# Turned queries and keys: two 64-partition sine products on VectorE, one cosine product on GpSimd

## The chip, the cores and the metric

The kernel runs on one core of one Trainium2 chip. The metric is the device time of one launch in microseconds, as the median of the runs. The profile is one further execution, recorded by the hardware profiler. The engines are TensorE (PE, with its weight load PEld), VectorE (DVE), ScalarE (ACT), GpSimd (POOL) and SyncE (SP).

## What is computed

One transformer layer over 2 x 1024 tokens of 256 channels, in float32: attention with 16 query heads and 4 key/value heads of 128, a layer norm of input plus attention, a mixture of 64 experts (6 for each token) with two shared ones, and a second layer norm. The change touches only the rotary turning of queries and keys in the attention:

```python
def _rotate_half(x):
    d = x.shape[-1] // 2
    return jnp.concatenate([-x[..., d:], x[..., :d]], axis=-1)
...
q = q * cos + _rotate_half(q) * sin
k = k * cos + _rotate_half(k) * sin
...
scores = jnp.einsum('bqhd,bkhd->bhqk', q, k) * scale
scores = jnp.where(causal[None, None], scores, jnp.finfo(scores.dtype).min)
attn = jax.nn.softmax(scores, axis=-1)
out = jnp.einsum('bhqk,bkhd->bqhd', attn, v).reshape(b, s, NH * HD)
```

Queries and keys lie turned on the chip: the 128 channels of a head on the partitions, 512 tokens along the row. The half rotation therefore swaps partitions 0 to 63 with 64 to 127.

## The kernel before

`attention` goes through 4 rounds of 64 steps. A step `n` takes one block of 128 queries of one head, for which `key_tiles(n)` key tiles of 128 count: 1 to 4 in the first 16 steps of every 32, 5 to 8 in the other 16. Every float32 matrix is split into a high part (rounded to fp32r, by ACT) and a low part (the rest), and each product is made of three matmuls: high by high, high by low, low by high.

Each engine has its own program, a loop over the steps written out by hand, and runs it in order; semaphores tie the engines together. In step `n` PE makes the scores of `n` (L606 to L611), transposes the probabilities of `n - 2` (L620), sums half of the outputs of a pair of blocks (the products of L539 to L541 into `o_ps`), and then has one "filling" of the single bank `proj_ps` (`fill`, L561, the same three lines): a projection of keys (K), queries (Q) or values (T), the turning back of values (V), or the output projection (O). `FILLS` gives the steps: modulo 16, K is filled at step 7, T at 3, V at 11; modulo 4, Q at 2, O at 0 and 1. The next filling waits until the bank is empty (`bank_free`): after O for `resid_added` (L504), after V for `v_split` (L516), after K and Q for `proj_taken` (L401). The outputs of step `n` (even) wait for `o_split` (`o_lo`, L476) and for `pt_split` (`pt_lo`, L468).

The turning of a K or Q filled at step `n`:

- ACT copies `proj_ps` to `taken` in step `n + 1` (L401).
- POOL multiplies `taken` by `cos` in step `n + 1` with two products of 64 partitions that swap the halves (L347, L349), so `turned` lies with its halves swapped; the weights that use it are swapped alike, on both sides of the scores, which leaves the scores as they are. Then POOL waits for the sine product and adds it (L353).
- DVE multiplies all 128 partitions of `taken` by `sin` in step `n + 2` (L490).
- ACT rounds `turned` to `q_hi` or `k_hi` in step `n + 3` (L428), and POOL makes `q_lo` or `k_lo` (L333).

DVE's order in a step is: `pt_lo` of step `n - 3` (L468); in even steps `o_lo` (L476); if `n % 4 == 1` the reciprocal of the row sums (L482); the sine product of a K or Q (L490); the two residual instructions of an O (L501); the maximum of the scores of `n` (L508); the low part of a V (L514). ACT's exponential (L391) needs the maximum, PE's transposes need the exponential. K's sine falls on step 9 of 16, Q's on every fourth step from 0, V's low part on step 12.

Of the kernel before, what the change touches and what calls it, by code (L numbers as in the profile page):

```python
# [26 lines left out]
ALU = mybir.AluOpType  # L27
ACT = mybir.ActivationFunctionType
AX = mybir.AxisListType
# [119 lines left out]
def now(k, per, n):  # L149


    return (k + 1) * per + n
# [10 lines left out]
def attention(nc, dram, resid, consts):  # L163
    with ExitStack() as ctx:
# [135 lines left out]
        def _(pool):  # L300
# [3 lines left out]
            pool.sem_inc(cos_made, 2 * len(ROPES))  # L304
            pool.sem_inc(turn_made, len(ROPES))
            pool.sem_inc(turn_split, len(ROPES))
            made = {"turn": len(ROPES), "split": len(ROPES)}
            for name, positions in (("x", SPLIT_X), ("w", SPLIT_W), ("wo", SPLIT_WO)):

                made[name] = SPLITS + sum(runs(at(positions, n), SPLITS, True, False) for n in range(FIRST, FIRST + STEPS))  # L310
# [14 lines left out]
            def body(k, first, last):  # L325
                for n in range(FIRST, FIRST + STEPS):
                    use = fill_at(n - 3)
                    if use and use[0] in "KQ" and runs(use[1], per(use[0]), first, last):

                        r = rope_of(*use)  # L330
                        hi, lo = turned_into(*use)
                        pool.wait_ge(turn_hi_made, now(k, len(ROPES), r + 1))
                        nc.gpsimd.tensor_tensor(lo, turned[r % 2][:], hi.bitcast(F32), ALU.subtract).then_inc(turn_split, 1)  # L333
                        made["split"] += 1
                    use = fill_at(n - 1)
                    if use and use[0] in "KQ" and runs(use[1], per(use[0]), first, last):

                        r = rope_of(*use)
                        pos = slice(half(*use) * HALF, (half(*use) + 1) * HALF)
                        pool.wait_ge(proj_taken, now(k, len(ROPES), r + 1))  # L340
                        pool.wait_ge(turn_made, made["turn"])
                        pool.wait_ge(turn_split, made["split"])
                        if not first:
                            pool.wait_ge(x_split, made["x"])
                            pool.wait_ge(w_split, made["w"])
                            pool.wait_ge(wo_split, made["wo"])
                        nc.gpsimd.tensor_tensor(turned[r % 2][0:64], taken[r % 2][64:128], cos[64:128, pos], ALU.mult).then_inc(cos_made, 1)  # L347
                        pool.wait_ge(cos_made, 2 * now(k, len(ROPES), r) + 1)
                        nc.gpsimd.tensor_tensor(turned[r % 2][64:128], taken[r % 2][0:64], cos[0:64, pos], ALU.mult).then_inc(cos_made, 1)  # L349
                        pool.wait_ge(cos_made, 2 * now(k, len(ROPES), r + 1))  # L350
                        made["turn"] += 1
                        pool.wait_ge(sin_made, now(k, len(ROPES), r + 1))
                        nc.gpsimd.tensor_tensor(turned[r % 2][:], turned[r % 2][:], turn_sin[r % 2][:],  # L353
                                                ALU.add).then_inc(turn_made, 1)
                    if not first:
                        lower_parts(pool, nc.gpsimd, k, n, first, last)
                        for name, positions in (("x", SPLIT_X), ("w", SPLIT_W), ("wo", SPLIT_WO)):
                            made[name] += runs(at(positions, n), SPLITS, first, last)
# [90 lines left out]
        def _(dve):  # L449
# [8 lines left out]

            def body(k, first, last):
                for n in range(FIRST, FIRST + STEPS):  # L460
# [11 lines left out]
                    if n % 2 == 0 and runs(j, PAIRS, first, last):  # L472
# [4 lines left out]
                                                ALU.subtract).then_inc(o_split, 1)  # L477
                    q = (n - 5) // 4
# [4 lines left out]
                    use = fill_at(n - 2)  # L483
                    if use and use[0] in "KQ" and runs(use[1], per(use[0]), first, last):

                        r = rope_of(*use)
                        pos = slice(half(*use) * HALF, (half(*use) + 1) * HALF)
                        dve.wait_ge(proj_taken, now(k, len(ROPES), r + 1))
                        dve.wait_ge(turn_made, now(k, len(ROPES), r - 1))
                        nc.vector.tensor_tensor(turn_sin[r % 2][:], taken[r % 2][:], sin[:, pos], ALU.mult).then_inc(sin_made, 1)  # L490
# [14 lines left out]
                    if runs(n, STEPS, first, last):  # L505

                        dve.wait_ge(scored, now(k, STEPS, n + 1))
                        nc.vector.tensor_reduce(neg_max[:, n % 4:n % 4 + 1], scores_ps[n % 2][:, score_cols(n)],  # L508
                                                AX.X, ALU.max, negate=True).then_inc(max_made, 1)
                    if use and use[0] == "V" and runs(use[1], per("V"), first, last):  # L510
# [5 lines left out]
                                                ALU.subtract).then_inc(v_split, 1)  # L516
                    if first:

                        lower_parts(dve, nc.vector, k, n, first, last)
# [947 lines left out]
```

## Time and profile before

| | us |
|---|---|
| median of 3 runs | 1422.31 |
| lowest, highest | 1422.07, 1423.52 |
| profiled execution | 1425.77 |
| its span in the trace | 1424.0 |
| PE busy | 1254.1 (88%) |
| DVE busy | 991.5 (70%) |
| ACT busy | 846.5 (59%) |
| POOL busy | 809.8 (57%) |

The attention lies in the first 60% of the span, the routing and the experts behind it. PE busy is the time in which a matmul was under way, with modelled ends; the pitch of the matmuls' starts says more of what PE did. A timeline lists an engine's instructions by start and duration; in square brackets stands idle time of the engine before the instruction, and what ended it. Instructions of DVE can start a little before their predecessor's recorded end.

### The profile page before, as it was taken

How to read it: one execution, taken by the hardware profiler on the slowest of the kernel's cores; microseconds unless marked ns; L12 is line 12 of the kernel's file. 1: busy time of each engine (PE TensorE's matmuls, PEld its weight loads, DVE VectorE, ACT ScalarE, POOL GpSimd, SP SyncE). 2: the span in 40 equal slices, each digit the busy share in tenths (PEclk: the TensorE clock that was granted, in tenths of full speed). 3: DMA queues.
4: the chain of work that ended last, by engine and by line, in shares of the span. 5: the costliest groups of instructions: out<-in, count | busy, mean ns of one | idle time of the engine just before them, and what ended most of it. 6: DMA issues, size and time to landing. Idle time of an engine off the chain costs nothing. (4 is left out here: it accounts for less than half of the span.)

```text
span 1424.0 us, 27954 instructions
## 1 busy us (share of the span) xinstructions
PE 1254.1 (88%) x8732; PEld 1117.1 (78%) x8732; DVE 991.5 (70%) x2012; ACT 846.5 (59%) x1875; POOL 809.8 (57%) x798
## 2 busy tenths in 40 slices
PE   3899999999999999999999997539925999999966
PEld 2789899899899899899899897536615999999954
DVE  2677677677677677777776777572204999999956
ACT  2666666566666566666665664622204989899932
POOL 4754754654754654754654630037774888888840
PEclk9999999999999999999999999559966999999979
DMA  6320040120040120140400001014225888888868
GB/s 224 116 76 1 11 153 23 57 76 1 21 151 15 57 76 1 27 150 11 122 1 2 1 1 34 1 49 104 104 101 172 263 260 262 257 263 263 267 204 269
DMA packets 100293, 151.29 MB, mean 106 GB/s; under 512 B 10410, under 2 KB 73038, under 8 KB 100196
## 3 DMA queue, kind: packets, MB, share of 16 engines
q1 hardware_dynamic: 89156, 124.75, 29.0%
q0 software_dynamic: 11040, 25.30, 5.3%
q8 instruction: 54, 0.88, 0.3%
q14 instruction: 43, 0.35, 0.1%
HBM read 92.51 MB, written 62.46 MB: 109 GB/s over the span
## 5 line engine op out<-in xcount | busy, mean ns | idle before, releaser
L508 DVE TENSOR_REDUCE neg_max<-scores 128x1 f32<-128x256 f32 (+7 forms) x256 | 192.6, 752 | 178.3 <-PE scores L611 178.1
L418 ACT ACTIVATE pt_hi<-pt 128x512 fp32r<-128x512 f32 (+3 forms) x384 | 174.8, 490 | 204.8 <-PE pt L620 201.7
L468 DVE TENSOR_TENSOR pt_lo<-pt,pt_hi 128x512 fp32r<-128x512 f32 (+3 forms) x384 | 200.8, 551 | 23.5 <-ACT pt_hi L418 21.6
L391 ACT ACTIVATE probs<-scores,neg_max 128x256 f32<-128x256 f32 (+7 forms) x256 | 190.1, 743 | 21.9 <-DVE neg_max L508 21.8
L539 PE MATMUL o_ps<-pt_hi,v_hi 128*128 128x256 f32 (+1 forms) x640 | 193.4, 302 | 4.9 <-DVE o_lo L476 4.8
L347 POOL TENSOR_TENSOR turned<-taken,cos 64x512 f32<-64x512 f32 x80 | 105.6, 1320 | 152.7 <-ACT taken L401 147.5
L540 PE MATMUL o_ps<-pt_lo,v_hi 128*128 128x256 f32 (+1 forms) x640 | 179.5, 281 | 0.0
L541 PE MATMUL o_ps<-pt_hi,v_lo 128*128 128x256 f32 (+1 forms) x640 | 179.1, 280 | 0.0
L620 PE MATMUL pt<-ident,probs 128*128 128x128 f32 x1152 | 168.2, 273 | 0.0
L1106 POOL DMA_INDIRECT results_dram<-y_sb,dest x134 | 145.2, 1083 | 32.8 <-issue 25.9
L611 PE MATMUL scores<-k_hi,q_lo 128*128 128x512 f32 (+4 forms) x384 | 151.5, 395 | 0.0
L333 POOL TENSOR_TENSOR q_lo<-turned,q_hi 128x512 fp32r<-128x512 f32 x64 | 82.6, 1291 | 113.9 <-ACT q_hi L428 113.9
L353 POOL TENSOR_TENSOR turned<-turned,turn_sin 128x512 f32<-128x512 f32 x80 | 103.8, 1298 | 72.7 <-DVE turn_sin L490 71.2
L752 POOL DMA_INDIRECT rows_dram<-rows,slots_int x96 | 94.2, 982 | 86.0 <-issue 86.0
L620 PEld LDWEIGHTS pt<-ident,probs 128*128 128x128 f32 x1152 | 134.9, 141 | 5.0
L606 PE MATMUL scores<-k_hi,q_hi 128*128 128x512 f32 (+4 forms) x384 | 132.1, 344 | 2.7 <-POOL q_lo L333 2.7
L607 PE MATMUL scores<-k_lo,q_hi 128*128 128x512 f32 (+4 forms) x384 | 131.1, 341 | 0.0
L539 PEld LDWEIGHTS o_ps<-pt_hi,v_hi 128*128 128x128 f32 x640 | 121.1, 189 | 10.2 <-issue 7.4
L540 PEld LDWEIGHTS o_ps<-pt_lo,v_hi 128*128 128x128 f32 x640 | 121.9, 191 | 0.0
L541 PEld LDWEIGHTS o_ps<-pt_hi,v_lo 128*128 128x128 f32 x640 | 121.2, 189 | 0.0
L501 DVE SCALAR_TENSOR_TENSOR resid<-proj_ps,row_inv,resid 128x256 f32<-128x256 f32 x256 | 110.7, 473 | 7.5 <-PE proj_ps L541 7.5
L349 POOL TENSOR_TENSOR turned<-taken,cos 64x512 f32<-64x512 f32 x80 | 105.8, 1323 | 6.3
(186 smaller groups left out, 3619.0 us busy)
## 6 DMA issues: line engine op xcount, KB each, us to landing
rows_dram<-empty SPq DMA_DIRECT2D x32, 919.1 KB
up_raw<-in_up SPq DMA_DIRECT2D x69, 368.0 KB, 3.9
x_in<-rows_dram SPq DMA_DIRECT2D x68, 258.0 KB, 3.5
parts<-results_dram SPq DMA_DIRECT2D x16, 768.0 KB, 9.8
down_raw<-in_down SPq DMA_DIRECT2D x69, 128.0 KB
down_raw<-in_down_tail SPq DMA_DIRECT2D x69, 112.0 KB
w_raw<-in_w SPq DMA_DIRECT2D x8, 768.0 KB, 9.1
x_raw<-in_xT SPq DMA_DIRECT2D x8, 512.0 KB, 5.0
```

The lines of the kernel that those rows point to most:

```text
L391: nc.scalar.activation(probs[:, m % 4, 0:w], scores_ps[m % 2][:, score_cols(m)], ACT.Exp, bias=neg_max[:, m % 4:m % 4 + 1], accum_out=row_ ...
L418: nc.scalar.activation(pt_hi[m // 2 % 2][:, a:z, P * (m % 2):P * (m % 2) + P], pt_ps[c % 2][:, 0:P * (z - a)].rearrange("p (k q) -> p k q" ...
L468: nc.vector.tensor_tensor(pt_lo[m // 2 % 2][part], pt_ps[c % 2][:, 0:P * (z - a)].rearrange("p (k q) -> p k q", q=P), pt_hi[m // 2 % 2][pa ...
L508: nc.vector.tensor_reduce(neg_max[:, n % 4:n % 4 + 1], scores_ps[n % 2][:, score_cols(n)], AX.X, ALU.max, negate=True).then_inc(max_made, 1)
L539: nc.tensor.matmul(out, lh, rh, start=first, stop=False)
L540: nc.tensor.matmul(out, lh, rl, start=False, stop=False)
L541: return nc.tensor.matmul(out, ll, rh, start=False, stop=last)
L606: nc.tensor.matmul(out, q_hi[b][qt], k_hi[u][:, keys], start=True, stop=False)
L607: nc.tensor.matmul(out, q_hi[b][qt], k_lo[u][:, keys], start=False, stop=False)
L611: mm = nc.tensor.matmul(out, q_lo[b][qt], k_hi[u][:, keys], start=False, stop=True)
L620: mm = nc.tensor.transpose(pt_ps[c % 2][:, (t - a) * P:(t - a + 1) * P], probs[:, m % 4, t * P:(t + 1) * P], ident[:])
L1106: pool.indirect_dma_start(out=dram["results"], out_offset=bass.IndirectOffsetOnAxis(ap=dest[buf][:, s:s + 1], axis=0), in_=y_sb[buf][:, s, ...
```

## The change

The sine products swap the halves and the cosine product does not, so `turned` lies straight. POOL makes one cosine product of 128 partitions in place of two of 64. DVE makes two sine products of 64 partitions in place of one of 128, each from the opposite half of `taken` and of `sin`. In DVE's order within a step, Q's sine keeps its place (the reciprocal now stands behind it, which never falls on the same step), K's sine moves behind the residual and the low part of V, and the maximum moves behind the low part of V and K's sine. POOL's extra waits for earlier sums and low parts are replaced by one wait on `turn_split`.

```diff
-            pool.sem_inc(cos_made, 2 * len(ROPES))
-            pool.sem_inc(turn_made, len(ROPES))
-            pool.sem_inc(turn_split, len(ROPES))
-            made = {"turn": len(ROPES), "split": len(ROPES)}
...
+            for s in (cos_made, turn_made, turn_split):
+                pool.sem_inc(s, len(ROPES))
...
                         pool.wait_ge(proj_taken, now(k, len(ROPES), r + 1))
-                        pool.wait_ge(turn_made, made["turn"])
-                        pool.wait_ge(turn_split, made["split"])
-                        if not first:
-                            pool.wait_ge(x_split, made["x"])
-                            pool.wait_ge(w_split, made["w"])
-                            pool.wait_ge(wo_split, made["wo"])
-                        nc.gpsimd.tensor_tensor(turned[r % 2][0:64], taken[r % 2][64:128], cos[64:128, pos], ALU.mult).then_inc(cos_made, 1)
-                        pool.wait_ge(cos_made, 2 * now(k, len(ROPES), r) + 1)
-                        nc.gpsimd.tensor_tensor(turned[r % 2][64:128], taken[r % 2][0:64], cos[0:64, pos], ALU.mult).then_inc(cos_made, 1)
-                        pool.wait_ge(cos_made, 2 * now(k, len(ROPES), r + 1))
-                        made["turn"] += 1
+                        pool.wait_ge(turn_split, now(k, len(ROPES), r - 1))
+                        nc.gpsimd.tensor_tensor(turned[r % 2][:], taken[r % 2][:], cos[:, pos], ALU.mult).then_inc(cos_made, 1)
+                        pool.wait_ge(cos_made, now(k, len(ROPES), r + 1))
                         pool.wait_ge(sin_made, now(k, len(ROPES), r + 1))
...
+            def turn_by_sine(k, kind, i):
+
+                r = rope_of(kind, i)
+                pos = slice(half(kind, i) * HALF, (half(kind, i) + 1) * HALF)
+                dve.wait_ge(proj_taken, now(k, len(ROPES), r + 1))
+                dve.wait_ge(turn_made, now(k, len(ROPES), r - 1))
+                nc.vector.tensor_tensor(turn_sin[r % 2][0:64], taken[r % 2][64:128], sin[64:128, pos], ALU.mult)
+                nc.vector.tensor_tensor(turn_sin[r % 2][64:128], taken[r % 2][0:64], sin[0:64, pos],
+                                        ALU.mult).then_inc(sin_made, 1)
+
...
+                    turn = fill_at(n - 2)
+                    if turn and turn[0] == "Q" and runs(turn[1], per("Q"), first, last):
+                        turn_by_sine(k, *turn)
                     q = (n - 5) // 4
...
-                    use = fill_at(n - 2)
-                    if use and use[0] in "KQ" and runs(use[1], per(use[0]), first, last):
-
-                        r = rope_of(*use)
-                        pos = slice(half(*use) * HALF, (half(*use) + 1) * HALF)
-                        dve.wait_ge(proj_taken, now(k, len(ROPES), r + 1))
-                        dve.wait_ge(turn_made, now(k, len(ROPES), r - 1))
-                        nc.vector.tensor_tensor(turn_sin[r % 2][:], taken[r % 2][:], sin[:, pos], ALU.mult).then_inc(sin_made, 1)
...
                         ins.then_inc(resid_added, 1)
-                    if runs(n, STEPS, first, last):
-
-                        dve.wait_ge(scored, now(k, STEPS, n + 1))
-                        nc.vector.tensor_reduce(neg_max[:, n % 4:n % 4 + 1], scores_ps[n % 2][:, score_cols(n)],
-                                                AX.X, ALU.max, negate=True).then_inc(max_made, 1)
...
+                    if turn and turn[0] == "K" and runs(turn[1], per("K"), first, last):
+                        turn_by_sine(k, *turn)
+                    if runs(n, STEPS, first, last):
+
+                        dve.wait_ge(scored, now(k, STEPS, n + 1))
+                        nc.vector.tensor_reduce(neg_max[:, n % 4:n % 4 + 1], scores_ps[n % 2][:, score_cols(n)],
+                                                AX.X, ALU.max, negate=True).then_inc(max_made, 1)
```

## Rows read from the trace of the kernel before

**Rows 1.** The page: busy time of each engine; PE's busy tenths in 40 slices.

```profile
PE 1254.1 (88%) x8732; PEld 1117.1 (78%) x8732; DVE 991.5 (70%) x2012; ACT 846.5 (59%) x1875; POOL 809.8 (57%) x798
...
PE   3899999999999999999999997539925999999966
```

**Rows 2.** The waits of PE, 25 to 880 us: total us, times, longest.

```profile
PE proj_ps L539 <- DVE v_lo L514: 11.9, 9, 1.4
PE proj_ps L539 <- DVE resid L501: 5.2, 8, 0.7
```

**Rows 3.** The timeline of PE in a light half: start us, duration us, engine, line.

```profile
267.94 0.27 PE L541 MATMUL o_ps<-pt_hi,v_lo 128*128 128x128 f32 x1
268.87 0.39 PE L539 MATMUL proj_ps<-wo_hi,o_hi 128*128 128x256 f32 x1 [0.65 <-DVE resid L501]
...
270.36 0.36 PE L539 MATMUL o_ps<-pt_hi,v_hi 128*128 128x256 f32 x1
...
277.30 0.39 PE L539 MATMUL proj_ps<-wo_hi,o_hi 128*128 128x256 f32 x1 [1.31 <-DVE v_lo L514]
```

**Rows 4.** The timeline of DVE over the same steps, 8 to 12.

```profile
264.59 1.45 DVE L490 TENSOR_TENSOR turn_sin<-taken,sin 128x512 f32<-128x512 f32 x1
...
267.06 0.96 DVE L490 TENSOR_TENSOR turn_sin<-taken,sin 128x512 f32<-128x512 f32 x1
267.95 0.86 DVE L501 SCALAR_TENSOR_TENSOR resid<-proj_ps,row_inv,resid 128x256 f32<-128x256 f32 x2
268.74 0.41 DVE L508 TENSOR_REDUCE neg_max<-scores 128x1 f32<-128x256 f32 x1
269.06 0.67 DVE L468 TENSOR_TENSOR pt_lo<-pt,pt_hi 128x512 fp32r<-128x512 f32 x1
269.66 0.41 DVE L476 TENSOR_TENSOR o_lo<-o_ps,o_hi 128x256 fp32r<-128x256 f32 x1
...
274.83 0.42 DVE L476 TENSOR_TENSOR o_lo<-o_ps,o_hi 128x256 fp32r<-128x256 f32 x1 [0.21 <-ACT o_hi L382]
275.17 1.27 DVE L490 TENSOR_TENSOR turn_sin<-taken,sin 128x512 f32<-128x512 f32 x1
276.37 0.28 DVE L508 TENSOR_REDUCE neg_max<-scores 128x1 f32<-128x128 f32 x1
276.57 0.68 DVE L514 TENSOR_TENSOR v_lo<-proj_ps,v_hi 128x512 fp32r<-128x512 f32 x1
```

**Rows 5.** The timeline of POOL over the same steps.

```profile
264.20 1.29 POOL L349 TENSOR_TENSOR turned<-taken,cos 64x512 f32<-64x512 f32 x1
266.18 1.29 POOL L353 TENSOR_TENSOR turned<-turned,turn_sin 128x512 f32<-128x512 f32 x1 [0.69 <-DVE turn_sin L490]
267.61 1.55 POOL L347 TENSOR_TENSOR turned<-taken,cos 64x512 f32<-64x512 f32 x1
...
274.62 1.28 POOL L347 TENSOR_TENSOR turned<-taken,cos 64x512 f32<-64x512 f32 x1 [0.22 <-issue]
```

**Rows 6.** The timeline of DVE in the experts: full and 48-partition instructions.

```profile
1161.38 0.41 DVE L1262 TENSOR_TENSOR hidden<-silu,gate_up 128x256 f32<-128x256 f32 x1
...
1163.36 0.43 DVE L1276 TENSOR_TENSOR hidden_hi<-hidden,hidden_hi 48x256 fp32r<-48x256 f32 x1
1163.82 0.69 DVE L1241 TENSOR_TENSOR xt_lo<-x_ps,xt_hi 128x512 fp32r<-128x512 f32 x1
```

**Rows 7.** The timeline of DVE in a heavy half, step 12.

```profile
332.17 0.68 DVE L490 TENSOR_TENSOR turn_sin<-taken,sin 128x512 f32<-128x512 f32 x1
```

**Rows 8.** The timeline of PE in the same heavy half.

```profile
334.51 0.28 PE L539 MATMUL proj_ps<-wo_hi,o_hi 128*128 128x256 f32 x1
```

**Rows 9.** The timeline of PE at the start of the attention.

```profile
34.22 0.47 PE L606 MATMUL scores<-k_hi,q_hi 128*128 128x128 f32 x1 [2.70 <-POOL q_lo L333]
...
41.93 0.50 PE L539 MATMUL proj_ps<-x_hi,w_hi 128*128 128x512 f32 x1 [0.72 <-ACT taken L401]
...
47.93 0.36 PE L539 MATMUL o_ps<-pt_hi,v_hi 128*128 128x256 f32 x1 [1.25 <-DVE o_lo L476]
```

More of the change, by code:

```diff
@@ L303, in _ @@
             pool.sem_inc(wo_split, SPLITS)
-            pool.sem_inc(cos_made, 2 * len(ROPES))
-            pool.sem_inc(turn_made, len(ROPES))
-            pool.sem_inc(turn_split, len(ROPES))
-            made = {"turn": len(ROPES), "split": len(ROPES)}
-            for name, positions in (("x", SPLIT_X), ("w", SPLIT_W), ("wo", SPLIT_WO)):
-                made[name] = SPLITS + sum(runs(at(positions, n), SPLITS, True, False) for n in range(FIRST, FIRST + STEPS))
+            for s in (cos_made, turn_made, turn_split):
+                pool.sem_inc(s, len(ROPES))
             pool.memset(ident[:], 0.0).then_inc(const_step, 1)
@@ L333, in body @@
                         nc.gpsimd.tensor_tensor(lo, turned[r % 2][:], hi.bitcast(F32), ALU.subtract).then_inc(turn_split, 1)
-                        made["split"] += 1
                     use = fill_at(n - 1)
@@ L356, in body @@
                         lower_parts(pool, nc.gpsimd, k, n, first, last)
-                        for name, positions in (("x", SPLIT_X), ("w", SPLIT_W), ("wo", SPLIT_WO)):
-                            made[name] += runs(at(positions, n), SPLITS, first, last)
             run_rounds(pool, body)
```

## The prediction

> **What bounds the kernel now.** I read the page first. TensorE (PE) is busy 88% of the span and 9 tenths or more in nearly every slice of the first 60% [rows 1]; that stretch, up to some 870 us, is the attention, and the change lies in it alone. So PE is the limit there, and a cost on VectorE (DVE) or GpSimd (POOL) counts only where it opens or closes a gap of PE, and the second view is the list of PE's waits in the attention [rows 2]: 11.9 us before a filling that waits for the low part of the values (L514), 5.2 us before one that waits for the residual (L501), nearly all else small. Third, PE's timeline. It repeats every 105.9 us: 16 steps over 1 to 4 key tiles (I call them the light half), then 16 over 5 to 8 (the heavy half). The heavy halves have no gap. Each of the eight light halves has four: 0.22 us at its step 6, 0.65 us at step 9 (residual), 1.31 us at step 12 (low values), 0.22 us at step 14; [rows 3] has the second and third, and where PE takes up the outputs of step 10 (270.36). The fourth view is the DVE and POOL timelines of the same microseconds, to see what makes these two gaps [rows 4, 5].
>
> At step 9 DVE runs reciprocal, the keys' sine (267.06 to 268.02), then the residual (to 268.81), and PE's second output filling starts at 268.87. At step 12 it runs the output's low part (to 275.25), a query sine of 1.27, a maximum of 0.28, then the low values (to 277.25), and PE starts at 277.30 [rows 3, 4].
>
> **The price of a sine product.** Alone it takes 0.68 [rows 7]. Beside a POOL product it is held up: at 264.59 the sine found a cosine running that ended at 264.20 + 1.29 = 265.49, and itself ended at 264.59 + 1.45 = 266.04, 0.55 later; at 267.06 it found the sum that ended at 266.18 + 1.29 = 267.47, and ended at 268.02, again 0.55 later [rows 4, 5]. So a sine that meets a running POOL product ends 0.55 after that one's end. The Trainium skill has a rule for this that speaks against the change (SBUF — State Buffer, "Who interferes with whom"): a VectorE instruction with two SBUF inputs and a GpSimd instruction that reads SBUF exclude one another for the whole instruction, and who issues first wins. The trace agrees except in the size: by the rule's letter the sine would need its whole 0.68 after the other's end, which would add 0.13 for each one blocked, 1 us in all below.
>
> **Half the partitions do not halve it.** On DVE, 48 partitions by 256 take 0.43 against 0.41 for 128 by 256 [rows 6]; on POOL, 64 partitions by 512 take 1.28 to 1.29, as 128 by 512 do [rows 5]. So I take 0.68 for each of the two sine products, and 1.29 for the one cosine that replaces two. There is also a hand-over. Ordinarily a DVE instruction starts 0.08 before its predecessor's end (276.57, behind a maximum that ended at 276.37 + 0.28 = 276.65). Where the starting partition changes it starts behind it: the 48-partition instruction that writes from partition 64 ends at 1163.36 + 0.43 = 1163.79, and the next starts at 1163.82 [rows 6]. The pair changes it three times, so from one instruction's end to the next one's start it takes 0.01 + 0.68 + 0.01 + 0.68 + 0.03 = 1.41, where one unblocked sine takes 0.68 - 0.16 = 0.52. The added 0.89 has as its lower bound a pair that costs as one does now (0), as upper bound two blocked products.
>
> **Query sines (64 of them).** They keep their place. In a light half's step 8, and where else the second cosine used to block them, the pair costs what the blocked one did: from 264.67 to 266.05 with no POOL product beside it, since POOL will have made its only cosine by 264.20, where its second one began; the old sine ended at 266.04. At steps 0 and 4 the pair delays a maximum by 0.2 to 0.9; ScalarE (ACT) then has idle time before its next copy, and the DVE stands idle 0.2 to 2 us within the next steps, so it is taken in. In the heavy half the DVE idles up to 2.9 us in a step. Its tightest place is the low values: sines unblocked from 332.25 on (the present one starts 0.08 before its predecessor's end), to 333.63, then 0.68 to 334.34 since the maximum now stands behind; PE wants them at 334.51 [rows 7, 8]. No gap, by 0.17.
>
> **Keys' sine in the light half, step 9 (8 times).** This decides. Taking it out from ahead of the residual ends the residual at 267.07 + 0.86 = 267.93, before PE asks for it at 267.94 + 0.27 = 268.21: the gap of 0.65 closes. But the pair now stands between the residual and the maximum, and behind that are two things that PE needs for its next outputs: a low part of the probabilities and o_lo. POOL's order is the query's sum (266.18 to 267.47, as before, since the query's sine ends as before), then the keys' cosine, 267.61 to 268.90. The first keys' product, ready at 267.94, finds it running: 268.90 + 0.55 = 269.45. The second: 270.14. Maximum 0.41 with its hand-over: 270.58. Low part of the probabilities 0.67, starting 0.08 early: 271.17. o_lo 0.41: 271.51. PE then starts its outputs at 271.54; it did at 270.36 [rows 3, 4]. So 0.65 is won at step 9, 1.83 is lost at step 10: **+1.18** each. Nothing gives it back: PE has no slack in which a delay can vanish. Bounds: if the pair were not blocked, 267.94 + 1.37 = 269.31, and the same chain ends at 270.71 (+0.35); if both were blocked, +0.6 more.
>
> **Low values, step 12 (8 times).** Out of its way goes a maximum of 0.28, and in its way comes one more sine. Its block vanishes too: POOL's cosine started only at 274.62 [rows 5], behind the keys' low part, and held the sine; with one cosine less per turn and PE 1.18 later, it ends before the DVE arrives. In PE's time: 275.25, products to 275.94 and 276.63, low values 276.66 to 277.34, PE at 277.39, against 277.30: **+0.09**. Bounds -0.2 (no hand-overs) and +0.6 (blocked).
>
> **The start (once).** Until the first scores PE waits for POOL's turning of the first queries, 2.70 us, and then for 0.72 and 1.25 more behind chains through POOL and ACT [rows 9]. One cosine (1.29) less in each of the first turns, minus blocked sines, makes the first sum end about 0.7 and the second about 2 us earlier. Of that little reaches PE at once: a sine pair ahead of the first maximum holds that to its old time within 0.15. At the gap of 0.72 the copy is then ready (-0.85 with it), at that of 1.25 a quarter is won. **-1.1**, bounds 0 and -3. The waits that POOL loses are met without stall in the rows I read; I count nothing.
>
> **Sum.** 8 x (1.18 + 0.09) - 1.1 = +9.1 us. The profiled execution took 1425.77 (1424.0 of span and 1.8 around it), 3.5 above the median of 1422.31; the same addition gives 1434.9 for such a one, and 1431.4 on the median.
>
> **Rivals.**
> A, the keys' pair is not held up (POOL's cosine comes earlier or lets it through): 8 x (0.35 + 0.09) - 1.1 = +2.4, 1424.7. For it: the pair misses the cosine's start by only 0.33 us. Against: three blocked sines in the rows, each by an instruction that had started first (the third: cosine to 275.90, sine to 276.44).
> B, the other side: a narrow product is short and passes the port. If it takes 0.34, the pair costs one present sine. Then step 10 starts as ACT allows, about 0.32 before 270.36, and the low values start when their high part is there, 0.6 earlier: 8 x -0.92 - 1.1 = -8.5, 1413.8. It decides from below some 0.45 us for one product. Against it are the rows of 48 and 64 partitions.
> C, the pair costs more than I count (both blocked, or a dearer hand-over), 0.3 for each: then the light half loses 0.6 more, and the heavy half's low values, with 0.17 to spare, open a gap of 0.13: 8 x 0.73 = +5.8 more, 1437.2.
>
> **Chances.** Forecast 0.60 (its own range 1428.5 to 1434), A 0.18, B 0.08, C 0.14. The range 1423.5 to 1436 leaves out B and the upper part of C. About 0.2%, 2.8 us, is what a measurement of this kernel can tell from no change: faster 0.09 (B and a little of A), same 0.19 (A and the foot of the forecast), slower 0.72.
>
> **What would show it.** In the profile after: the sine line with 160 instructions near 0.68, one of them near 1.5 in each light half, at step 9; the wait for the residual gone from PE's list; the wait for o_lo or the probabilities' low part at step 10 near 1.8 us, eight times; the wait for the low values still some 1.3. I am wrong if the step 10 gap is below 1 us (A), if sine products of 64 partitions take clearly less than 0.68 (B), or if heavy halves show gaps (C).

## The result, and the profile after the change

| | before | after |
|---|---|---|
| median of four runs, us | 1422.91 (1422.07 to 1424.34) | 1445.38 (1442.94 to 1447.28) |
| ratio, 95% interval | | 1.015 (1.0139 to 1.0162) |
| profiled execution, us (its span) | 1425.77 (1424.0) | 1442.94 (1441.2) |
| VectorE (DVE) busy, us | 991.5 | 1031.1 |
| GpSimd (POOL) busy, us | 809.8 | 700.7 |
| last maximum of the attention starts at, us | 869.22 | 888.77 |

The change costs 22.5 us on the medians, where +9.1 was forecast. The direction was right, the forecast size was 40% of the measured one, and 1445.38 lies outside the range, which ended at 1436.

The page after says where not to look. Its engine row answers to that in [rows 1]:

```profile
PE 1260.4 (87%) x8732; PEld 1120.1 (78%) x8732; DVE 1031.1 (72%) x2092; ACT 851.5 (59%) x1875; POOL 700.7 (49%) x718
```

POOL has 80 instructions and 109 us less, DVE 80 instructions and 40 us more, TensorE (PE) the same 8732 matmuls. Yet PE's busy time went up by 6.3 us: the same matmuls became longer. That one number is the first sign of what the prediction left out.

**The gaps.** The list of PE's waits, 100 to 850 us, which holds seven light halves (total us, times, longest). Before:

```profile
PE proj_ps L539 <- DVE v_lo L514: 9.2, 7, 1.3
PE proj_ps L539 <- DVE resid L501: 4.5, 7, 0.7
PE o_ps L539 <- DVE o_lo L476: 3.1, 14, 0.2
```

After:

```profile
PE o_ps L530 <- DVE o_lo L470: 15.7, 21, 1.8
PE proj_ps L530 <- DVE v_lo L498: 10.2, 7, 1.5
PE proj_ps L530 <- DVE resid L490: 1.1, 7, 0.2
```

The residual's wait of 0.65 at step 9 is gone, as forecast. In its place stands one of 1.80 for the output's low part at step 10: 15.7 - 3.1 = 12.6 us in seven halves. The low values at step 12 went from 1.31 to 1.46. And a wait of 0.17 for a residual is new. PE's gaps in one repeat of 32 steps are now 0.22 + 1.80 + 1.46 + 0.22 + 0.17 = 3.87 us, against 0.22 + 0.65 + 1.31 + 0.22 = 2.40 before: +1.47 each. The last of them, 0.17, stands at step 17, the second step of the heavy half.

**The chain behind the large gap.** Timeline of DVE after (start us, duration us, engine, line); it answers to [rows 4]:

```profile
269.25 0.86 DVE L490 SCALAR_TENSOR_TENSOR resid<-proj_ps,row_inv,resid 128x256 f32<-128x256 f32 x2
270.14 1.35 DVE L449 TENSOR_TENSOR turn_sin<-taken,sin 64x512 f32<-64x512 f32 x1
271.51 0.69 DVE L450 TENSOR_TENSOR turn_sin<-taken,sin 64x512 f32<-64x512 f32 x1
272.23 0.42 DVE L506 TENSOR_REDUCE neg_max<-scores 128x1 f32<-128x256 f32 x1
272.57 0.68 DVE L462 TENSOR_TENSOR pt_lo<-pt,pt_hi 128x512 fp32r<-128x512 f32 x1
273.17 0.41 DVE L470 TENSOR_TENSOR o_lo<-o_ps,o_hi 128x256 fp32r<-128x256 f32 x1
```

Timeline of POOL at the same time, behind the queries' sum:

```profile
269.67 1.28 POOL L336 TENSOR_TENSOR turned<-taken,cos 128x512 f32<-128x512 f32 x1
```

The first product of the keys starts while the cosine runs, which ends at 269.67 + 1.28 = 270.95, and ends itself at 270.14 + 1.35 = 271.49, 0.54 later. The second takes 0.69, and the maximum, the probabilities' low part and o_lo follow without a hole until 273.58. PE takes up the outputs at 273.73. This is the chain that the prediction wrote down, instruction by instruction.

**What was not in it.** PE in the same step, after, across the gap and beyond:

```profile
273.73 0.36 PE L530 MATMUL o_ps<-pt_hi,v_hi 128*128 128x256 f32 x1 [1.80 <-DVE o_lo L470]
...
274.52 0.47 PE L530 MATMUL proj_ps<-x_hi,w_hi 128*128 128x512 f32 x1
274.79 0.63 PE L531 MATMUL proj_ps<-x_lo,w_hi 128*128 128x512 f32 x1
```

The same matmuls in the kernel before:

```profile
271.15 0.40 PE L539 MATMUL proj_ps<-x_hi,w_hi 128*128 128x512 f32 x1
271.39 0.40 PE L540 MATMUL proj_ps<-x_lo,w_hi 128*128 128x512 f32 x1
```

Matmuls of 128x512 start 0.24 apart and last 0.40 before; after, they last 0.63, and the seven from 274.79 to 277.35 start 0.42 to 0.43 apart. The clock that TensorE was granted explains it. The page does not show it: its row for the granted clock, in tenths over 40 slices of 36 us, reads 9 for nearly the whole attention in both kernels, since a fall of 3.4 us takes only 0.05 from a slice (before, then after):

```profile
PEclk9999999999999999999999999559966999999979
PEclk8999999999999999999999999559976999999979
```

Windows view after (stretch, its length, busy us of PE, PEld, DVE, ACT, POOL with counts, then the granted clock as a share of full speed, DMA share, GB/s):

```profile
56.00:60.00 4.00, 3.02 (x17) 2.44 (x18) 2.28 (x6) 2.57 (x7) 3.36 (x3) 1.00 0.74 204
274.00:278.00 4.00, 4.00 (x16) 2.92 (x14) 1.03 (x3) 1.60 (x4) 2.26 (x3) 0.59 0.00 0
383.00:387.00 4.00, 4.00 (x16) 2.96 (x15) 1.11 (x4) 1.69 (x4) 2.38 (x3) 0.62 0.00 0
...
820.00:824.00 4.00, 4.00 (x29) 3.40 (x29) 1.88 (x5) 2.32 (x6) 2.92 (x3) 1.00 0.02 4
```

Column PEclk is the reading: 0.59 and 0.62 where it was 1.00 at the same place before. PE is busy all 4.00 us in the last three rows, but makes 16 matmuls in two of them and 29 in the third. Behind the 1.8 us gap the clock goes down from 2.4 to 1.2 GHz for 3.4 us and comes back. It does so in six of the eight light halves of this execution (from about 165, 275, 384, 493, 602 and 712 us), and not in the first and the last, whose gap is as long. Before, it never does between 40 and 880 us. From one light half to the next the work repeats every 105.9 us before, every 107.5 after where the clock holds (105.9 and 1.47 make 107.4), and every 109.1 to 109.2 where it falls, so a fall costs 1.6 to 1.7 us, half of the 3.4 that it lasts.

**The account**, on the last maximum of the attention in the two profiled executions. The start of the attention came out 2.5 us earlier. The gaps add 8 x 1.47 = 11.8. Six falls of the clock add 6 x 1.7 = 10.2. Sum +19.5; the trace has 888.77 - 869.22 = +19.55. (Taken from the repeats instead, 1.6 for each gap sum and 1.6 for each fall, the same account gives +19.9.) The rest of the program, which the change does not touch, was 2.4 us shorter in this one execution, which makes +17.2 on the spans.

### The profile page after: what moved, and what is told of

It is laid out like the page before. It is cut to its first block and busy times, and to the rows that moved or that the text cites. A ratio compares the mean times of both kernels' runs of the same rounds, so it can differ in the third digit from the quotient of the medians.

```text
span 1441.2 us, 27801 instructions
## 1 busy us (share of the span) xinstructions
PE 1260.4 (87%) x8732; PEld 1120.1 (78%) x8732; DVE 1031.1 (72%) x2092; ACT 851.5 (59%) x1875; POOL 700.7 (49%) x718
## 5 line engine op out<-in xcount | busy, mean ns | idle before, releaser
L336 POOL TENSOR_TENSOR turned<-taken,cos 128x512 f32<-128x512 f32 x80 | 104.2, 1302 | 162.0 <-ACT taken L385 162.0
L530 PE MATMUL proj_ps<-x_hi,w_hi 128*128 128x512 f32 x192 | 81.2, 423 | 16.4 <-DVE w_lo L251 12.4
```

The source lines that it names most:

```text
L530: nc.tensor.matmul(out, lh, rh, start=first, stop=False)
```

## The experiments

Gaps are PE's, in one light half, by step. On the chip of the first four runs the kernel before took 1493.79 us, because the part behind the attention was some 70 us longer there (623.8 us behind the last maximum in the trace of the order alone, 554.8 in that of before). The attention was not: with the order alone its last maximum comes 2.7 us before that of before. The changed kernel itself was not run on that chip. So for these runs the ratio and the gaps are what can be compared. "Last maximum" always stands against 869.22.

### The products alone, in the old order

```diff
                     turn = fill_at(n - 2)
-                    if turn and turn[0] == "Q" and runs(turn[1], per("Q"), first, last):
-                        turn_by_sine(k, *turn)
...
                         nc.vector.reciprocal(row_inv[:, cols], row_sum[:, cols]).then_inc(inv_made, 1)
+                    if turn and turn[0] in "KQ" and runs(turn[1], per(turn[0]), first, last):
+                        turn_by_sine(k, *turn)
```

(The maximum moves back ahead of the low values too.)

> The changed products (two sines of 64 partitions, one cosine) in VectorE's order of before: keys' pair ahead of the residual, maximum ahead of the low values. Theory 1 (stall plus clock): what costs is where the keys' pair stands and that GpSimd holds it up, and a PE gap near 2 us lets TensorE's granted clock fall to half for some 3.4 us, another 1.7 us. Here the pair stands before the residual: first product held by GpSimd's sum (to 268.0 in the microseconds of before), second by the cosine (to 269.7), residual to 270.6, so a gap near 2.3 at step 9 and none at step 10: 1.7 us per light half more than before, 0.4 more at the low values, and the clock falls in 6 to 8 light halves: 1445 to 1453 us. Theory 2 (the order is what costs, the products are free): within 1 us of before, 1423. Theory 3 (the products cost by VectorE's load, wherever they stand): as the changed kernel, 1445, with the gap spread over several steps.

Measured: 1530.55, ratio 1.0244 (1.0211 to 1.0276). The list of PE's waits, 100 to 850 us:

```profile
PE proj_ps L528 <- DVE resid L490: 18.5, 13, 2.5
PE proj_ps L528 <- DVE v_lo L503: 15.1, 14, 1.7
PE o_ps L528 <- DVE o_lo L470: 2.7, 12, 0.2
```

And the keys' pair (DVE) with PE behind it:

```profile
387.59 0.90 DVE L449 TENSOR_TENSOR turn_sin<-taken,sin 64x512 f32<-64x512 f32 x1
388.50 1.66 DVE L450 TENSOR_TENSOR turn_sin<-taken,sin 64x512 f32<-64x512 f32 x1
...
391.12 0.39 PE L528 MATMUL proj_ps<-wo_hi,o_hi 128*128 128x256 f32 x1 [2.50 <-DVE resid L490]
```

Here both products are held up, the first by POOL's sum, the second by its cosine (0.90 and 1.66), which was the prediction's upper bound for a pair. The gap of step 9 is 2.50 and that of step 12 is 1.65; a heavy half has one of 0.50 for the low values, where [rows 8] had none. So the two products are the dear part of the change, and the new order makes them cheaper than they would be. The clock falls here nine times: behind the 2.50 gap in six of eight cases, and behind the 1.65 gap in three of eight. The account closes again: the waits of 100 to 850 us sum to 36.3 us here and 16.8 before, 2.79 more in each light half, so 8 x 2.79 + 9 x 1.7 - 0.8 (start) = +36.8; the last maximum is at 906.10, +36.9. Theory 1 had the place and nearly the size of the large gap (2.3), but not the falls behind the gap of 1.65 nor the gap in the heavy half, and +2.4% is above the +1.6 to +2.2% that its times stood for. Theories 2 and 3 are out.

### The order alone, with the old products

```diff
-                    use = fill_at(n - 2)
-                    if use and use[0] in "KQ" and runs(use[1], per(use[0]), first, last):
+                    turn = fill_at(n - 2)
+                    if turn and turn[0] == "Q" and runs(turn[1], per(turn[0]), first, last):
...
+                    turn = fill_at(n - 2)
+                    if turn and turn[0] == "K" and runs(turn[1], per(turn[0]), first, last):
```

> The kernel before with the new order alone: one sine of 128 partitions, two cosines; keys' sine behind the residual, maximum behind the low values. Theory 1: the single keys' sine meets the first cosine, ends at 269.45, o_lo at 270.8, so a gap of 1.1 at step 10 in place of 0.65 at step 9; low values earlier by 0.2; the clock stays up, as it did in before at gaps of 1.3: 8 x 0.3 = +2.4, 1423 to 1427 us. Theory 2 (the order costs): near the changed kernel, 1440 to 1446, with a gap of 1.8 at step 10. Theory 3: as before, 1423.

Measured: 1492.56, ratio 0.9998 (0.9989 to 1.0008), no difference. Waits of PE, 100 to 850 us, and the keys' sine:

```profile
PE o_ps L547 <- DVE o_lo L476: 10.9, 21, 1.1
PE proj_ps L547 <- DVE v_lo L509: 5.2, 7, 0.7
...
371.58 1.60 DVE L519 TENSOR_TENSOR turn_sin<-taken,sin 128x512 f32<-128x512 f32 x1
```

Gaps: none at step 9, 1.12 at step 10, 0.74 at step 12: 2.30 in all against 2.40. The last maximum is 2.7 us earlier, 2.0 of it from the start and 0.1 from each repeat. Theory 1 had the gap at step 10 right; what it put at 0.2 for the low values came out as 0.57, and with it the +2.4 us went. The order swaps a wait of 0.65 for one of 1.12, and gains 0.57 at step 12. Even one sine behind the residual is held up by a cosine (1.60). The clock never falls in the attention from 40 us on. The two halves of the change are therefore about nothing for the order, and +2.4% for the products, which the order brings down to +1.5%.

### The step 10 gap filled with matmuls

```diff
-                        for c0, c1 in spans:
+                        for c0, c1 in spans * (4 if n % 32 == 10 else 1):
```

The scores of step 10 are computed four times over, some 2 us of needless PE work exactly where PE stands idle.

> The changed kernel, and in step 10 of each light half PE makes the scores of the block four times in place of once, each time from the start, so the output is the same. That is some 1.7 us of additional matmuls, put where PE stands idle for 1.8 us. Theory 1: the idle time goes, nothing is later, the granted clock stays at full speed and the matmuls of steps 10 and 11 keep their pitch: 10 to 14 us less than the changed kernel, 1431 to 1436 us, although PE does more. Rival (the clock falls for another reason, as the load of all engines or a fixed interval): the clock falls as often as in the changed kernel and the time is 1444 to 1448.

Measured: 1506.65, ratio 1.0087 (1.007 to 1.0104), against 1.015 and 1.0137 for the changed kernel itself. PE's waits, then two windows of 6 us across the place where the clock fell:

```profile
PE o_ps L530 <- DVE o_lo L470: 3.1, 14, 0.2
...
171.00:177.00 6.00, 4.68 (x35) 4.23 (x36) 5.19 (x13) 3.47 (x9) 4.91 (x3) 1.00 0.20 35
275.00:281.00 6.00, 4.54 (x37) 4.00 (x36) 4.66 (x10) 3.28 (x9) 2.56 (x2) 1.00 0.00 1
```

The gap is gone, the clock holds from 40 us on, and by its ratio the kernel with more work is half a percent faster: 12.9 us above before, within the 9 to 14 that theory 1 gave, where the changed kernel was 22.5 and 18.5 above on its two chips. The last maximum comes 10.7 us after that of before, 1.6 for each light half with 2.1 off at the start: as a step 10 that is just as late, without the fall. This separates the two costs. The delay of step 10 is DVE's chain and stays when PE is kept busy; the rest of the loss hangs on PE standing idle.

### The same, half as much

```diff
-                        for c0, c1 in spans:
+                        for c0, c1 in spans * (2 if n % 32 == 10 else 1):
```

> As the run that made the scores of step 10 four times, but twice: some 0.55 us more matmuls, so PE idles about 1.25 us there, with everything else of the changed kernel. Theory 1: the clock stays up, and the light half costs nothing more than in the changed kernel less the 1.7 us of the slow matmuls. Rival: any idle time beyond that of before lets the clock fall; then it falls as often as in the changed kernel.

Measured, one run: 1436.44 against 1424.35. PE's waits:

```profile
PE o_ps L530 <- DVE o_lo L470: 11.3, 21, 1.2
```

The gap is 1.17, the clock does not fall, and the last maximum comes at +11.4, about 1.6 for each half. The delay is that of the changed kernel, and only the idle part of it is shorter.

### The changed kernel once more

The same kernel without an edit, on another chip, to see whether the falls are a property of a place in the program.

> The changed kernel once more, beside the kernel before on the same chip, as the measure for the two that follow. Expected: gaps of 1.8 us at step 10 of all eight light halves, a fall of the granted clock behind at least five of them, and 1.3 to 1.6% over before.

Measured: 1442.89 (1440.57 to 1447.49), ratio 1.0137 (1.0115 to 1.016). The gaps are the same (PE's waits), and the windows behind two of them are not:

```profile
PE o_ps L530 <- DVE o_lo L470: 15.8, 21, 1.8
...
276.00:280.00 4.00, 4.00 (x15) 2.88 (x15) 0.79 (x3) 1.27 (x3) 2.71 (x3) 0.60 0.00 0
384.00:388.00 4.00, 3.61 (x22) 3.05 (x23) 2.10 (x6) 2.18 (x6) 3.32 (x4) 1.00 0.00 0
```

The clock fell behind three of the eight gaps (at 168, 277 and 601 us), where it was six the first time; at least five were expected. The light half at 384 had a fall in one execution and none in the other. So a fall follows a gap of this length in some cases, in varying places. The account: start -0.9, gaps +11.8, three falls +5.1, sum +16.0; measured 885.73 - 869.22 = +16.5. A varying number of falls would also make the runs of this kernel spread more, and they do: 7 us here and 4 in the first comparison, against 2.2 to 2.3 for the kernel before in both comparisons. That the falls are what spreads them is not shown, since only one execution on each chip has a trace.

### The keys' product made narrow

```diff
-                        turn_by_sine(k, *turn)
+                        turn_by_sine(k, *turn, width=8 if n % 32 == 9 else HALF)
```

The keys' sine products of the light halves cover 8 of 512 columns; the other 504 are left out.

> The changed kernel, with the keys' two sine products of the light halves (step 9) on 8 of their 512 columns: 504 columns of the keys' sine product are left out there. Theory 1: the gap at step 10 goes from 1.8 to 0.2 to 0.4, the clock does not fall: 8 x 1.5 + 10 to 14 us less than the changed kernel, 1418 to 1423 us; the low values' gap stays near 1.45. Theory 3 (load of VectorE by all the pairs): most of the loss stays, 1435 to 1445, since 64 of 80 pairs are as in the changed kernel.

Measured: 1497.63, ratio 1.002 (1.001 to 1.003). POOL's cosine, the pair, and PE at step 10:

```profile
373.91 1.29 POOL L336 TENSOR_TENSOR turned<-taken,cos 128x512 f32<-128x512 f32 x1
374.38 0.85 DVE L449 TENSOR_TENSOR turn_sin<-taken,sin 64x8 f32<-64x8 f32 x1
375.24 0.16 DVE L450 TENSOR_TENSOR turn_sin<-taken,sin 64x8 f32<-64x8 f32 x1
376.93 0.35 PE L530 MATMUL o_ps<-pt_hi,v_hi 128*128 128x256 f32 x1 [0.77 <-DVE o_lo L470]
```

The gap falls from 1.80 to 0.77, and the clock holds in all eight halves, so the keys' pair makes the larger part of this gap, and theory 3 is out. But a gap of 0.2 to 0.4 was expected, and 1418 to 1423 us where before had 1422.3; the ratio stands 0.2% above 1. The expectation took nearly the whole of the pair's time as gone, and the first product, narrow as it is, still waits for the cosine, which ends at 375.20. This shows the hold-up by itself: the free narrow product takes 0.16, the one behind the cosine 0.85, so the hold-up costs 0.69. For the full product it costs 1.35 - 0.69 = 0.66, so it has little to do with its size. The gap of 1.46 at step 12 stays, as it should.

### POOL's cosine behind the keys' products

```diff
                         pool.wait_ge(turn_split, now(k, len(ROPES), r - 1))
+                        if use[0] == "K":
+                            pool.wait_ge(sin_made, now(k, len(ROPES), r + 1))
                         nc.gpsimd.tensor_tensor(turned[r % 2][:], taken[r % 2][:], cos[:, pos], ALU.mult).then_inc(cos_made, 1)
```

> The changed kernel; GpSimd's cosine product of the keys now waits for VectorE's two sine products of the keys, so they can't be held up by it (the cosine itself and the sum come about 0.6 us later). This prices the hold-up: the forecast put it at 0.83 us per light half (+1.18 held up, +0.35 not). Theory 1: the gap at step 10 goes from 1.8 to 1.0 to 1.1, the clock stays up (it stayed up at gaps of 1.1 to 1.5 in the runs so far): 8 x 0.8 + 10 to 14 us less than the changed kernel, 4 to 8 us over before. Rival: the hold-up isn't what fills the gap, the gap stays above 1.6 and the time within 3 us of the changed kernel.

Measured: 1430.09 (1428.97 to 1431.72), ratio 1.0038 (1.0024 to 1.0052). DVE, POOL and PE:

```profile
375.81 0.69 DVE L451 TENSOR_TENSOR turn_sin<-taken,sin 64x512 f32<-64x512 f32 x1
376.51 0.68 DVE L452 TENSOR_TENSOR turn_sin<-taken,sin 64x512 f32<-64x512 f32 x1
...
377.37 1.27 POOL L338 TENSOR_TENSOR turned<-taken,cos 128x512 f32<-128x512 f32 x1 [1.99 <-DVE turn_sin L452]
...
378.73 0.36 PE L532 MATMUL o_ps<-pt_hi,v_hi 128*128 128x256 f32 x1 [1.13 <-DVE o_lo L472]
```

Both products are free, the gap of step 10 is 1.13, and the clock does not fall. The hold-up is worth 1.81 - 1.13 = 0.68 for each light half, where the sum of the prediction had 0.83; the pair, even free, behind the residual costs the rest. With one wait, 12.8 us of the changed kernel's loss are gone: 8 x 0.68 = 5.4 of it is the shorter gap. The other 7.4 lie between what three falls and six falls of 1.7 us cost (5.1 and 10.2), and the time is in the 4 to 8 us over before that theory 1 gave.

### The keys' turning taken apart and made later

The runs so far say what is wanted: the new order, no hold-up, and POOL's work of the keys out of step 9. This version takes the old products in the new order; the keys' first cosine waits for their sine, the second cosine and the sum go behind the queries' low part, one step later, and k_hi and k_lo two steps later.

```diff
-                    use = fill_at(n - 3)
-                    if use and use[0] in "KQ" and runs(use[1], per(use[0]), first, last):
+                    for kind, back in (("Q", 3), ("K", 3 if first else 5)):
+                        use = fill_at(n - back)
+                        if use and use[0] == kind and runs(use[1], per(kind), first, last):
...
+                        if kind == "K" and not first:
+                            pool.wait_ge(sin_made, now(k, len(ROPES), r + 1))
+                        if 0 in halves:
+                            nc.gpsimd.tensor_tensor(turned[r % 2][0:64], taken[r % 2][64:128], cos[64:128, pos], ALU.mult).then_inc(cos_made, 1)
+                        if 1 in halves:
```

> A version meant to beat both. The products of before (one sine of 128 partitions, two cosines), the new order of VectorE, and the keys' turning taken apart so that it is in nobody's way: GpSimd's first cosine of the keys waits for VectorE's sine (no hold-up), the second cosine and the sum come behind the queries' low part, and ScalarE's rounding and GpSimd's low part of the keys come two steps later (step 12 in place of 10). Expected: gap at step 10 from 1.1 (with the new order alone) to 0.2 to 0.3, low values' gap 0.8 to 1.1: 0.7 us less than before per light half and 2 us less at the start, if that holds: 1 to 6 us under before. Rival: the later sum of the keys pushes GpSimd's next cosine or ScalarE's copies into the way, and the low values' gap or the wait for the queries' low part grows by as much: within 1 us of before.

Measured: 1421.52 (1418.7 to 1423.44, ten runs) against 1424.35, ratio 0.9979 (0.997 to 0.9989). PE's waits, 100 to 850 us:

```profile
PE proj_ps L560 <- DVE v_lo L522: 8.7, 7, 1.3
PE o_ps L560 <- DVE o_lo L489: 4.6, 21, 0.2
```

Steps 6, 10 and 14 have 0.22 each, step 12 has 1.25: 1.91 against 2.40 before. It is faster than the kernel before by 0.2%, which is small, but its interval leaves out 1. The low values' gap came out above the 0.8 to 1.1 expected, the time within the range. One fall of the clock is in its attention from 40 us on, at 64 us, behind a low-values gap that was 1.61 long in this first half. The account: 8 x -0.49 - 2.1 (start) + 1.7 (one fall) + 0.36 (that longer gap) = -4.0; measured 865.22 - 869.22 = -4.0. Some 1.2 of the start's 2.1 belong to this execution and not to the kernel: the next version differs from this one nowhere before step 11, and its step 8 comes only 0.8 earlier than before (see on the start below). The medians, -2.8 us, carry the result.

### The same with the queries' cosine of step 11 behind its sine

Against the version before this one:

```diff
-                        if kind == "K" and not first:
+                        if (kind == "K" or n % 16 == 11) and not first:
```

> The version before this one (keys turned late), and GpSimd's cosine products of the queries filled at step 10 wait for VectorE's sine of step 12, so that the sine, and the low values behind it, are not held up. In the trace of that version the sine ends at 380.34 in place of 379.61 and the low values 0.6 us later than they could. Theory: the gap at step 12 goes from 1.25 to 0.7, the queries' sum comes some 0.8 us later and makes ScalarE's rounding and the outputs of step 14 late by 0.2 to 0.4: 0.2 to 0.4 us less per light half, 1 to 3 us below that version, 0.3 to 0.4% below before. Rival: the later sum makes step 14's gap (0.22) grow by 0.5 or more: no gain.

Measured: 1424.25 against 1424.02, ratio 1.0004 (0.9995 to 1.0014). PE's waits:

```profile
PE o_ps L560 <- DVE o_lo L489: 11.4, 21, 1.2
PE proj_ps L560 <- DVE v_lo L522: 5.2, 7, 0.7
```

Step 12 went from 1.25 to 0.74, and step 14 from 0.22 to 1.20. The wait bought 0.51 and cost 0.98 two steps later. The chain to it, POOL's sum for the queries, then ACT and DVE:

```profile
383.52 1.29 POOL L365 TENSOR_TENSOR turned<-turned,turn_sin 128x512 f32<-128x512 f32 x1
384.91 0.63 ACT L441 ACTIVATE q_hi<-turned 128x512 fp32r<-128x512 f32 x1 [0.87 <-POOL turned L365]
385.84 0.42 DVE L489 TENSOR_TENSOR o_lo<-o_ps,o_hi 128x256 fp32r<-128x256 f32 x1 [1.08 <-ACT o_hi L394]
```

The held-back cosines make the sum late, ACT stands idle 0.87 us for it, and o_hi, which is behind q_hi in ACT's order, and with it o_lo and the outputs are late. That is the expectation's mechanism, but with the rival's size; the rival came out, and the version before this one stays the best.

## Why the prediction was right in part, and wrong in size

**The keys' pair at step 9: right.** The residual's gap closed (0.65 to 0). The forecast lost 1.83 at step 10; the gap is 1.80 (1.80 to 1.82 in every light half of both traces of this kernel). The first product ends 0.54 after the cosine where 0.55 was read from three blocked sines. Rival A, that the pair is not held up, is shut out by the 1.35 of its first product. Undoing the hold-up alone gave 0.68, where the sum had 1.18 - 0.35 = 0.83, so with a free pair the gap is 1.13 where the bound gave 1.00.

**No halving: right.** A free product of 64 partitions takes 0.69 on DVE, the one cosine of 128 partitions on POOL 1.28. Rival B is out.

**The low values: right in kind, 0.15 instead of 0.09.** Together with the keys' pair that is +1.30 against +1.27.

**The query sines "taken in": failed at one place.** The prediction called the low values the tightest place of the heavy half, with 0.17 to spare. Those held; the gap opened elsewhere, at the residual behind the pair of step 16, which I had not laid on the timeline. There was no slack there: before, DVE's residual ended at 288.68 + 0.84 = 289.52 and PE took it at 289.57, as soon behind it as at step 9, where PE stood waiting (268.81 and 268.87). After, a query pair with its second product at 291.96 and its maximum at 292.68 goes ahead of it:

```profile
291.96 0.69 DVE L450 TENSOR_TENSOR turn_sin<-taken,sin 64x512 f32<-64x512 f32 x1
...
293.96 0.85 DVE L490 SCALAR_TENSOR_TENSOR resid<-proj_ps,row_inv,resid 128x256 f32<-128x256 f32 x2
294.87 0.39 PE L530 MATMUL proj_ps<-wo_hi,o_hi 128*128 128x256 f32 x1 [0.17 <-DVE resid L490]
```

From the end of o_lo to the start of the maximum the pair takes 1.46 with its hand-overs where the blocked sine took 1.27; with no slack, the 0.19 more is nearly all in the gap of 0.17 that the trace shows, eight times: 1.3 us in all. A gap in the heavy half was one of the prediction's signs of rival C. Its cause is not that of C, a pair dearer by 0.3: this one takes 1.46 where 1.41 was counted. The wrong step was that a query pair costs what the blocked sine before it did.

**The start: right sign, size unsettled.** Forecast -1.1. The maximum of step 8 came 2.5 us earlier in the first trace of the changed kernel and 0.9 earlier in the second. The two differ in the clock and not in the kernel: in the first, matmuls of 128x512 start 0.23 us apart from 16.3 to 19.6 us, the high level, and in the second, as in the kernel before, 0.43 apart there and on to about 39 us, the low level. The two other traces with such an early high stretch, the order alone and the best version, start 2.0 and 2.1 us earlier; of the six others five start 0.7 to 1.3 earlier, around the forecast, and one 2.1. So part of the first trace's 2.5 is probably the early clock and not the change; no run separates them.

**The step that failed: "Nothing gives it back", and with it the sum 8 x (1.18 + 0.09) - 1.1.** They priced a gap of PE at its own length and looked only for what could make it shorter. They named nothing that could make it dearer: the clock granted behind it stood in the sum at nothing, without a reason. The lengths of the gaps account for 11.8 - 2.5 = +9.3 at the last maximum, next to the forecast of +9.1; that near match is partly luck, since it has 1.3 for the residual of step 17 against a start that was earlier than forecast. What is missing is the granted clock: 10.2 us in one trace, 5.1 in the other. In the kernel before the clock held from 40 to 880 us with gaps of up to 1.32; the forecast made a gap of 1.83, longer than any in that stretch, and I did not ask what the clock would do. The 2.70 of [rows 9] is longer still, but it is no evidence for a clock that holds: it stands at 34 us, where TensorE was at the low level already (128x512 matmuls 0.43 apart until 39.4 us, 0.23 from 39.8 us). The range was too narrow for the same reason: it took in the bounds of DVE's times and none for PE's.

The experiments bear this cause out from four sides. (Falls and gaps are counted from 40 us on.) Filling the gap with needless matmuls ends the falls and takes the ratio from 1.0137 or 1.015 to 1.0087. Filling it in part, in one run, does the same to the falls. Making it shorter from DVE's side (0.77 with a narrow product, 1.13 with the cosine behind) does too. And where gaps are longer (2.50 and 1.65 in the old order), there are nine falls. Counted over all traces: behind gaps of 1.6 to 2.5 us the clock fell in 6 of 8, 3 of 8, 6 of 8, 3 of 8 and 1 of 1 cases; behind gaps of up to 1.46 us, which stand eight times in each of six traces, in none. The Trainium skill says (TensorE: Matmul & The Clock Gate, "What's actually happening") that the clock follows how busy the engine has lately been, with the low level as the default. The traces agree in that every one of the 19 falls begins within 1.6 us of the end of a gap of 1.6 us or more, and in that all traces begin at the low level (128x512 matmuls 0.43 us apart at 13 us); which of two equal gaps brings a fall, that sentence does not tell.

**Against the medians.** The attention gives about +16 to +20 us in the two traces of this kernel, the medians +22.5 on one chip and +18.5 on the other. Some 2 to 3 us more are not placed: the profiled execution of the first comparison was itself the fastest of its four, and the number of falls varies from one execution to the next.

**Open.** Why the clock falls behind one gap of 1.8 us and not behind the next. Of the low values' 1.25 us in the best version 0.51 is a sine that is held up; what could take away the other 0.74 was not tried. The changed kernel's own products in the schedule of the best version were not tried.

## What to carry to other kernels

A gap of the bound engine has a second price beside its length. Where a change makes one on TensorE longer than any that the trace of before shows at the high clock, put a fall of the granted clock into the sum, with the extra time that the matmuls behind it would take at half speed, or at least into the range; and read the clock in windows of a few us, since the tenths of the page did not show six falls. And where a GpSimd product holds up a VectorE one, the cost is nearly the rest of the running one (0.66 and 0.69 of 0.8 us here) and hardly depends on the size of the one that waits; an added wait on GpSimd can let the other by first, but look at who needs the product that it holds back, since the wait won 12.8 us at one place here and moved a gap by two steps at another. Last, work "taken in" by idle time must be laid on the timeline at every step that it touches; the place with 0.17 of slack held, the one with none did not.

## What the runs showed of the hardware that I had not expected

- With an idle gap of 1.80 us in otherwise full work, the granted clock went from 2.4 to 1.2 GHz in 6 of 8 and in 3 of 8 cases, at about 1.7 us each. With gaps of 1.46 and below, in the same stretch of the attention, it never did.
- Some 2 us of needless matmuls in such a gap, eight times, made the kernel faster: ratio 1.0087 instead of 1.0137 to 1.015.
- A product of 64 x 8 elements took 0.85 us beside a running POOL product and 0.16 beside none.
- The held-up products of 64x512 end 0.54 to 0.55 us after the POOL product's end, less than the 0.69 that they take when free, so a part of them does run beside it; the one of 64x8 ends 0.03 after it, where it takes 0.16 free.
